# Attention stage: the first quarter of the odd unit's transposes is evicted by ScalarE in every second pair

## What is computed

```python
# src is 2 x 2048 x 512; 16 heads of width 32; attention_bias is 2 x 16 x 2048 x 2048
q = (x @ Wq + bq).reshape(B, S, N_HEAD, HEAD_DIM).transpose(0, 2, 1, 3)
k = (x @ Wk + bk).reshape(B, S, N_HEAD, HEAD_DIM).transpose(0, 2, 1, 3)
v = (x @ Wv + bv).reshape(B, S, N_HEAD, HEAD_DIM).transpose(0, 2, 1, 3)
scores = jnp.einsum('bhqd,bhkd->bhqk', q / math.sqrt(HEAD_DIM), k)
scores = scores + attention_bias
scores = jnp.where(src_mask, -jnp.inf, scores.astype(jnp.float32))
probs = jax.nn.softmax(scores, axis=-1).astype(v.dtype)
ctx = jnp.einsum('bhqk,bhkd->bhqd', probs, v)
...
x = x + (ctx @ Wo + bo)
h = _ln(x) * g2 + beta2
ff = _gelu2(h @ W1 + b1) @ W2 + b2
return x + ff
```

## Time and profile before

| | us |
|---|---|
| time, median of 3 runs | 3628.09 (3627.71 to 3628.99) |
| the profiled execution, its own time | 3630.03 |
| its span, from the first to the last instruction | 3627.9 |
| busy in the span: PE / DVE / ACT / POOL | 3566.8 / 2261.2 / 2181.8 / 2057.5 |
| mean granted clock of TensorE in the span | 0.990 |

### The profile page before, as it was taken

The page is one execution under the profiler, slowest core; times in us unless marked ns, Lnnn a source line. Parts: engine busy times, 40 slices in busy tenths (PEclk is TensorE's granted clock), DMA queues, the critical chain, the costliest instruction groups (busy, mean ns, idle before and its releaser), DMA issues. The chain is left out here.

```text
span 3627.9 us, 79714 instructions
## 1 busy us (share of the span) xinstructions
PE 3566.8 (98%) x31987; PEld 2449.2 (68%) x31987; DVE 2261.2 (62%) x4509; ACT 2181.8 (60%) x3039; POOL 2057.5 (57%) x778
## 2 busy tenths in 40 slices
PE   7999999999999999999999999999999999999999
PEld 3444468888888888888888888887444444444444
DVE  7676668888888888888888888887211111121102
ACT  2343369999999999999999999997110210111110
POOL 1111169889899989899999898896310110120100
PEclk8999999999999999999999999999999999999998
DMA  5555498888998888988888988887300110110002
GB/s 194 197 185 195 181 395 325 321 330 323 351 368 324 320 323 329 383 336 328 324 318 338 383 323 326 326 324 258 119 23 12 35 35 3 44 58 31 28 24 93
DMA packets 209989, 828.35 MB, mean 228 GB/s; under 512 B 25044, under 2 KB 58964, under 8 KB 134360
## 3 DMA queue, kind: packets, MB, share of 16 engines
q1 hardware_dynamic: 204404, 814.83, 59.6%
q10 hardware_dynamic: 5220, 8.42, 0.6%
HBM read 731.93 MB, written 91.23 MB: 227 GB/s over the span
## 5 line engine op out<-in xcount | busy, mean ns | idle before, releaser
L1199 POOL TENSOR_TENSOR at_tiles<-at_tiles,at_negmask 128x1792 f32<-128x1792 f32 x509 | 1827.7, 3634 | 193.9 <-DMA at_tiles<-in_bias 181.1
L1289 ACT ACTIVATE at_tiles<-at_tiles,at_rmin 128x2048 f32<-128x2048 f32 x512 | 1025.2, 2002 | 56.5 <-DVE at_rmin L1336 55.9
L1235 PE MATMUL at_ps_p<-consts,at_tiles 128*128 128x128 f32 x8192 | 1025.4, 272 | 0.1
L1235 PEld LDWEIGHTS at_ps_p<-consts,at_tiles 128*128 128x128 f32 x8192 | 930.5, 142 | 37.4 <-ACT at_prob_t L1297 0.4
L1297 ACT ACTIVATE at_prob_t<-at_ps_p 128x512 f32<-128x512 f32 x1536 | 831.9, 596 | 129.7 <-PE at_ps_p L1235 128.0
L1336 DVE CUSTOM_DVE_ANT_0 at_tiles<-at_ps_s,at_tiles 128x1024 f32<-128x1024 f32 x512 | 624.6, 1220 | 117.3 <-PE at_ps_s L1216 114.0
L1216 PE MATMUL at_ps_s<-at_k_stack,at_q_stack 128*128 128x512 f32 x2048 | 677.7, 432 | 5.1 <-DVE at_rmin L1336 3.3
L1336 DVE CUSTOM_DVE_ANT_0 at_tiles<-at_ps_s,at_tiles,at_rmin 128x1024 f32<-128x1024 f32 x512 | 657.7, 1285 | 19.3 <-PE at_ps_s L1222 1.0
L1252 PE MATMUL at_ps_c<-at_prob_t,at_v 128*32 128x128 f32 x16384 | 500.3, 274 | 0.6 <-DVE at_ctx_rows L1354 0.6
L1252 PEld LDWEIGHTS at_ps_c<-at_prob_t,at_v 128*32 128x32 f32 x16384 | 431.6, 110 | 43.7 <-issue 43.0
L1583 PE MATMUL ff_ps_m<-ff_norm_t,ff_w 128*128 128x512 f32 x1024 | 443.7, 594 | 0.5 <-ACT ff_feats L1723 0.5
(11 more groups left out here) (187 smaller groups left out, 2597.6 us busy)
## 6 DMA issues: line engine op xcount, KB each, us to landing
at_tiles<-in_bias SPq DMA_DIRECT2D x512, 1024.0 KB, 7.1
at_k_stack<-k_hi SPq DMA_DIRECT2D x128, 256.0 KB, 5.2
at_k_stack<-k_lo SPq DMA_DIRECT2D x128, 256.0 KB, 5.2
negm<-em_mask_out SPq DMA_DIRECT2D x32, 512.0 KB, 6.6
at_q_stack<-q_hi SPq DMA_DIRECT2D x128, 128.0 KB, 5.0
at_q_stack<-q_lo SPq DMA_DIRECT2D x128, 128.0 KB, 5.1
at_v<-v SPq DMA_DIRECT2D x64, 256.0 KB, 8.0
at_negmask<-negm SPq DMA_DIRECT2D x32, 512.0 KB, 9.7
```

Source lines behind the costliest of these rows:

```text
L1199: pool.tensor_tensor(tiles[s][:, 0:PCOLS], tiles[s][:, 0:PCOLS], negm[s][:, 0:PCOLS], ALU.add).then_inc(s_pool, 1)
L1235: last = pe.transpose(ps_p[k][:, y * P:(y + 1) * P], tiles[s][:, t * P:(t + 1) * P], ident)
L1289: act.activation(tiles[s][:, :], tiles[s][:, :], ACT.Exp, bias=rmin[:, s, 1:2], scale=-1.0, accum_out=rsum[:, s:s + 1]).then_inc(s_exp, 1)
```

## The change

In odd pairs, `take(u + 1, 0)` leaves DVE's list and enters ACT's list right behind `exp(u + 2)`. Even pairs stay as they are. Nothing else is changed: the same 2048 chunks are copied to the same places, and PE, POOL and SP keep their instructions and their order.

```diff
@@ in the ScalarE block of attention_stage
                         take(u, c)
                     if u + 2 < NU:
                         exp(u + 2)
+                    if p % 2 == 1:
+                        take(u + 1, 0)
                     take(u + 1, 2)
                     take(u + 1, 3)
...
@@ in the VectorE block of attention_stage
                 if p < NP:
                     take(u, 3)
-                    take(u + 1, 0)
+                    if p % 2 == 0:
+                        take(u + 1, 0)
                 if u + 3 < NU:
                     scores(u + 3, 0)
```

## The result

The changed kernel takes 3766.05 us (median of 4 runs, 3764.22 to 3767.59) against 3627.9 for the kernel before (3627.04 to 3628.99): 3.8% slower, ratio 1.0378 with a 95% interval of 1.0366 to 1.0390. The forecast was 3772 us, in a range of 3750 to 3795. The profiled execution took 3767.59 us, its span 3765.5, which is 137.6 more than the span before.

The account below looks back on a forecast made before the run. PE was taken to bound the kernel. 127 odd-pair stalls of 1.14 us add 144.8 us and relief at the stage's beginning removes 1, so the median 3628.1 + 143.8 = 3772 us, range 3750 to 3795 (chance 0.84).

Parts of the forecast that it names:

- PE is the pace: Mid-attention: PE busy 500.00 of 500 us, a pair taking 7.94 us, while ACT, POOL and DVE have slack.
- The chain from chunk (u, 2) through the exponential to chunk (u + 1, 3): Odd pairs: chunk, ACT copy, exponential, next copy, PE's chunk follow in sequence, so the stall recurs in every odd pair.
- The deficit: Odd pair: ACT's copy ends at 1517.78 but PE wants the bank at 1516.79, so 0.99 us late.
- The way from ACT's end to PE's start: Delay from copy end to PE's waiting transpose: taken as 0.15 us, lower bound 0.06, giving a stall of 1.14.
- the microsecond of relief at the start: Beginning of attention: DVE's lost copies shorten PE's waits for DVE's minimum, 1 us taken of at most 3.3.
- The signs: Profile after: PE busy about 465 of 500 us, waiting 145 us for ACT; DVE's odd-pair wait up 0.6 + 1.1 us.
- The number of stalls: Odd pairs of attention: 128 of 256, less the last, which has no exponential, so 127 stalls.
- The covers: ACT's extra 0.48 us per odd pair fits its 0.70 us waiting per pair; copies queued behind are needed later.
- The clock did not fall: Rival, chance 0.06: PE's stalls lower its clock, about 1.7 us each, up to 3988 us.
- ScalarE as the bound of the even pairs: Rival, chance 0.05: the exponential behind an odd pair is 0.48 us late, PE waits, adding 61 us: 3833 us.
- absorption: Rival, chance 0.03: POOL and the bias DMA set the pace, the stall only moves a wait: 3625 us, no slowdown.
- The clearly shorter stall: Rival, chance 0.02: PE's wait is released before the copy's recorded end, giving from 3742 us.

## Why the prediction was right

**That PE is the pace** was right: PE is again busy for 500.00 of 500 us in both kernels that move the copy ahead of the exponential, and within 2.3 us of the time before, whatever ScalarE and VectorE carry.

**The chain from chunk (u, 2) through the exponential to chunk (u + 1, 3)** was right, link by link. ACT waits 0.32 us for the chunk (0.33 before), the exponential starts 0.49 behind its copy, the next copy starts 1.99 behind that and ends after 0.58.

**The deficit** of 0.99 us before the way to PE: after, the copy ends 1510.63 - 1509.66 = 0.97 late.

**The way from ACT's end to PE's start** was the term that I mis-sized. I took 0.15, from a row of the embedding stage, and called 0.06, a row of VectorE, its lower bound. It measured 1510.69 - 1510.63 = 0.06. I had left out the restart as perhaps one slow record; it is real: the four transposes behind the stall take 0.66 together, where four took 0.60 before the change, and the matmuls that open the next pair start 0.06 later for it. The deficit itself was 0.02 too large. So a stall is worth 0.97 + 0.06 + 0.06 = 1.09 us, the 9.03 - 7.94 of the windows, and not 1.14. By 127 that is 138 us, against 144.8 forecast and a growth of the span of 137.6. The 0.05 per stall, 6 us in all, is the difference between 3772 and 3766. That it is so small is in part luck: the way was 0.09 too long and the missing restart 0.06 too short, and they took most of each other away. Of the microsecond of relief at the start, nothing can be shown: PE's waits for VectorE's minimum went from 3.3 to 3.0 us, and they were 4.0 to 4.3 in the three kernels that relieve VectorE without a stall.

**The signs.** Two that it named came out smaller, for one reason: it put PE's idle time equal to the 1.14 us of lateness, and the idle time is only 0.87. So PE was busy for 474.56 of 500 us and not for about 465, and its wait came to 111.1 us and not to 145. The growth of VectorE's wait in an odd pair, 0.6 + 1.1 us by the prediction, was 2.12 - 0.42 = 1.70.

**The number of stalls**, 127, was exact. The prediction's lower bound is off by a rounding: 127 x 1.05 is 133, as it says first, and not the 132 of its range.

**The covers** held: ScalarE's added copy (all copies ahead of the exponential: no loss), the copies queued behind it, and the even pairs, which kept 7.94. The 49.5 us in the sum of ScalarE's waits is a line that the earlier trace rows doesn't show, from 600 to 2500 us:

```profile
ACT at_tiles L1289 <- DVE at_rmin L1336: 49.5, 233, 0.6
```

**The rivals.** The clock did not fall, neither here nor with the longer stall of 1.36 us. The Trainium skill's rule on cycling through PSUM banks ("TensorE: Matmul & The Clock Gate", section "A second HAM failure mode: psum-queue depth-cycling") does not show here: the granted clock is 1.00 in mid-attention with 127 stalls and with 255. ScalarE as the bound of the even pairs is refuted, and so is absorption: twice the stalls cost twice the time. The clearly shorter stall did not come either: PE starts 0.06 us behind the copy's recorded end, not ahead of it. That ScalarE's copy is the cheaper one (0.58 against 0.69 us) changed nothing, since no copy's duration was on the path in the good place.

## What to carry to other kernels

Where one engine is busy all the time, moving a buffer's release to another engine is safe only if that engine comes to it before the busy one wants the buffer again. Compare two times in the timeline: when the waiting engine wants it, and when the instruction ahead of the release in the new queue ends; here an exponential of 2 us stood between them, and the free share of ScalarE (9%) said nothing about it. Read the lateness from start to start, since the idle time of a pipelined engine understates it (0.87 for 1.03 us here).

## What the runs showed of the hardware

- A VectorE addition with both operands in SBUF takes 0.42 us, or up to 3.83 when it starts while POOL is in an addition of its own (209 of 512), and then ends about 0.28 behind it. The copies and passes that read PSUM kept their 0.69 and 1.22 us in the same kernel.
- TensorE's clock stayed at its upper level, granted 1.00, with 0.88 us of idle time in each pair of 9 us and with 1.36 in every second one. It was at the lower level, 0.50, from 1516 to 1520 us of the kernel with VectorE's mask additions, where PE stood still for 3.35 us until 1516.99.
- The way from the end of a copy to the start of the matmul that waits for it was 0.06 us from ScalarE and 0.05 from VectorE (1514.88 to 1514.93).
- A shorter matmul of 128 instead of 256 columns brought its successor's start forward by 0.05 us, but in one of two places the matmul after that successor did not move.
